# Routed experts: the last two tiles of each expert as one group of 256 moving rows

## What is computed

```python
h = _L0_tok_ref(x, ...)                    # gelu(codebook[x] @ W1 + b1) @ W2 + b2, 256 -> 1024 -> 256
h = h + _L0_attn_ref(_layernorm(h), ...)   # two minGRU layers, a scan over the sequence
h = h + _L0_ffn_ref(_layernorm(h), ...)    # below

def geglu(x, w1, w2, w3):
    return jax.nn.gelu(x @ w1, approximate=False) * (x @ w2) @ w3
shared = geglu(xf, w1s, w2s, w3s)
idx = jnp.argmax(xf @ Wg, axis=-1)         # one of 8 experts per token
for e in range(N_EXPERTS):
    y = geglu(xf, W1[e], W2[e], W3[e])
    final = final + jnp.where((idx == e)[:, None], y, 0.0)
```

## Time and profile before

| what | value |
|---|---|
| median of 3 runs | 494.27 us (494.14 to 494.92) |
| profiled execution: its own time | 494.67 us |
| profiled execution: span of the trace | 492.9 us |
| TensorE busy | 485.4 us, 98% |
| VectorE busy | 326.5 us, 66% |
| ScalarE busy | 248.9 us, 50% |
| GpSimd busy | 71.7 us, 15% |

### The profile page before, as it was taken

The page is one execution under the profiler, slowest core; times in us unless marked ns, Lnnn a source line. Parts: engine busy times, 40 slices in busy tenths (PEclk is TensorE's granted clock), DMA queues, the critical chain, the costliest instruction groups (busy, mean ns, idle before and its releaser), DMA issues.

```text
span 492.9 us, 8768 instructions
## 1 busy us (share of the span) xinstructions
PE 485.4 (98%) x2790; PEld 419.5 (85%) x2791; DVE 326.5 (66%) x538; ACT 248.9 (50%) x380; POOL 71.7 (15%) x85
## 2 busy tenths in 40 slices
PE   8999999999999999999999999999999999999997
PEld 7889888888888887888888788888888888888886
DVE  2567768669676778767544877843857476657364
ACT  3776774574663563534443765534554457254321
POOL 4431031011011001104350001011001000101120
PEclk9999999999999999999999999999999999999999
DMA  4852021001030004001354465530556074500352
GB/s 131 311 205 71 23 65 43 21 23 43 23 97 1 1 0 148 25 0 44 129 174 105 152 231 205 197 112 32 193 173 229 21 243 156 197 32 26 108 200 85
DMA packets 22986, 52.71 MB, mean 107 GB/s; under 512 B 6224, under 2 KB 16464, under 8 KB 18992
## 3 DMA queue, kind: packets, MB, share of 16 engines
q1 hardware_dynamic: 17296, 42.39, 25.1%
q0 software_dynamic: 2640, 7.22, 4.3%
q10 hardware_dynamic: 3024, 2.75, 1.9%
HBM read 41.85 MB, written 10.51 MB: 106 GB/s over the span
## 4 chain that ended last, share of the span: by engine, by line
PE 86%; DVE 4%; DMA 4%; ACT 3%; issue 2%; SPq 1%; POOL 0%; POOLq 0%; DVEq 0%
PE ps L258 23%; PE ps L259 22%; PE ps L260 22%; PE ps L733 8%; PE ps L736 4%; PE ps L745 3%; DMA stage<-w1s_in 2%; PE ps L640 1%; DVE stats L1107 1%; PE ps L558 1%; DMA q<-codebook_in,idx_sb 1%; PE ps L593 1%; PE ps L605 1%; DVE v_gate L1138 1%; ACT a_gate L893 1%
## 5 line engine op out<-in xcount | busy, mean ns | idle before, releaser
L1042 DVE TENSOR_TENSOR hT<-ps,hT 128x512 fp32r<-128x512 f32 x64 | 43.9, 686 | 34.6 <-ACT hT L833 17.6
L1385 DVE TENSOR_TENSOR w_slots<-stage,w_slots 128x2048 f32 x24 | 54.8, 2288 | 15.2 <-ACT w_slots L974 15.0
L258 PE MATMUL ps<-w_slots,xTp 128*128 (+1 forms) x160 | 64.0, 400 | 0.2
L260 PE MATMUL ps<-w_slots,xTp 128*128 (+1 forms) x160 | 62.4, 390 | 0.0
L259 PE MATMUL ps<-w_slots,xTp 128*128 (+1 forms) x160 | 62.4, 390 | 0.0
L733 PE MATMUL ps<-w_slots,gTp 128*128 (+1 forms) x160 | 58.9, 408 | 0.0
L432 POOL DMA_INDIRECT y_tokens<-y_row,row_ids x23 | 23.1, 1006 | 198.4 <-DVE y_row L1408 187.1
L844 ACT ACTIVATE hT<-ps 128x512 fp32r<-128x512 f32 x32 | 19.2, 598 | 54.5 <-DVE ps L1048 54.5
L1366 DVE TENSOR_TENSOR g_buf<-ps,gelu_buf 128x512 f32<-128x512 f32 x40 | 26.8, 685 | 28.1 <-PE ps L260 28.1
L736 PE MATMUL ps<-w_slots,gTp 128*128 (+1 forms) x160 | 44.9, 281 | 0.0
L974 ACT ACTIVATE w_slots<-stage 128x2048 f32 x21 | 40.3, 1918 | 3.9 <-issue 3.9
(11 more groups left out here) (185 smaller groups left out, 1218.1 us busy)
## 6 DMA issues: line engine op xcount, KB each, us to landing
stage<-ew_in SPq DMA_DIRECT2D x24, 1024.0 KB, 5.3
x_sorted<-zero_row SPq DMA_DIRECT2D x25, 128.5 KB, 2.5
x_row<-x_sorted ACTq DMA_DIRECT2D x21, 128.0 KB, 2.1
stage<-w1s_in SPq DMA_DIRECT2D x2, 1024.0 KB, 8.4
fetched<-y_tokens SPq DMA_DIRECT2D x4, 512.0 KB, 5.4
out_rows<-fetched SPq DMA_DIRECT2D x3, 512.0 KB, 2.9
first_stage<-tok_w_in SPq DMA_DIRECT2D x1, 1024.0 KB, 5.0
first_stage<-tok_w_in SPq DMA_DIRECT2D x4, 256.0 KB, 4.2
```

The lines of the kernel that those rows point to most:

```text
L258: pe.matmul(dst, lhs_hi, rhs_hi, start=start, stop=False, skip_group_check=shares_bank)
L260: return pe.matmul(dst, lhs_lo, rhs_hi, start=False, stop=stop, skip_group_check=shares_bank)
L1042: dve.tensor_tensor(hT[:, c % RING, 1, :], ps[:, bank, :], f32(hT[:, c % RING, 0, :]), ALU.subtract).then_inc(h_lo, 1)
L1385: dve.tensor_tensor(w_slots[:, bass.ds(to + (PART + c * WCH), WCH)], stage[:, c, :], f32(w_slots[:, bass.ds(to + c * WCH, WCH)]), ALU.subt ...
```

## The change

Each expert now has at least two tiles (`steps[:, :, 0:2] = -1`), and its last two are one window of 256 rows that is computed like the shared layer: weights stationary, 256 rows moving, the hidden values transposed from the start. A window has four pairs p of hidden chunks; `window_up` is 24 products of 256 columns for one p, `window_down` four pairs of a 512 and a 256 column product. Tiles beyond two (`count` of them, "singles") keep the old form, in nested conditions. The loop now runs over experts, two per turn, and turns behind the last up products, so that `window_down` of p = 2 and 3 is issued in the next expert. Addresses in `w_slots` are constants. Output rows have two buffers, and a new semaphore `y_free` tells VectorE that the store before the last has landed. `XT` becomes 2 x 8 + 14 = 30; GpSimd's loop runs over `XT` as before.

```diff
-    XT = TILES + EXPERTS - 1
+    MORE = TILES - 2
+    XT = 2 * EXPERTS + MORE
...
             def to_tokens(i):
                 pool.indirect_dma_start(
                     out=y_tokens, out_offset=bass.IndirectOffsetOnAxis(ap=row_ids[:, i:i + 1].bitcast(I32), axis=0),
-                    in_=y_row[:], in_offset=None,
+                    in_=y_rows[:, i % 2 * D:(i % 2 + 1) * D], in_offset=None,
                     bounds_check=(TILES + 1) * P - 1, oob_is_err=True).then_inc(y_stored, 16)
 
 
             pool.wait_ge(ids_land, 16)
             for i in range(XT):
-                pool.wait_ge(y_taken, i + 1)
+                pool.wait_ge(y_taken, i + 2)
                 if i:
                     pool.wait_ge(y_stored, i * 16)
+
+                pool.sem_inc(y_free, 1)
                 to_tokens(i)
 
 
...
+
+            w_parts = w_slots[:].rearrange("p (s h n) -> p s h n", s=2, h=2)
+
+            def window_up(e, p, odd):
+
+                slot = 0 if odd else SLOT
+                for w, done in enumerate((wa_ps, wb_ps)):
+                    for c in range(2):
+                        for k in range(KD):
+                            o = slot + w * WCH + k * HID + (2 * p + c) * P
+                            last = mm3(pe, ps[:, p % 2 * 2 + w, c * WINDOW:(c + 1) * WINDOW], w_slots[:, o:o + P],
+                                       w_slots[:, o + PART:o + PART + P], xW[:, odd, 0, k, :], xW[:, odd, 1, k, :],
+                                       k == 0, k == KD - 1)
+                    last.then_inc(done, 1)
+
+            def window_down(rounded, p, odd):
+
+                side = 0 if odd else 1
+                pe.wait_ge(w_lo, rounded)
+                for i in range(2):
+                    for c in range(2):
+                        o = 2 * WCH + (2 * p + c) * D
+                        cols = slice(c * WINDOW + i * P, c * WINDOW + (i + 1) * P)
+                        pe.matmul(ps[:, 4 + i, :].rearrange("p (h n) -> p h n", h=2), hW[:, p, 0, cols],
+                                  w_parts[:, side, :, o:o + D], start=p == 0 and c == 0, stop=False, skip_group_check=True)
+                        last = pe.matmul(ps[:, 4 + i, 0:D], hW[:, p, 1, cols], w_slots[:, side * SLOT + o:side * SLOT + o + D],
+                                         start=False, stop=p == PAIRS - 1 and c == 1, skip_group_check=True)
+                    if p == PAIRS - 1:
+                        last.then_inc(tile_done, 1)
+
...
+
+            def expert(e, odd):
+
+
+                opening = isinstance(e, int) and e == 0
+                if opening:
+                    chunk_down(AHEAD - 2, 0)
+                else:
+                    window_down(e * PAIRS - 1, PAIRS - 2, not odd)
+                s = ahead_of(pe, e)
+                m = rows_of(pe, e)
+                pe.wait_ge(pair_lo, e + 1)
+                if not opening:
+                    one_transposes(m)
+                pe.wait_ge(split_lo, e * 3 + 5)
+                window_up(e, 0, odd)
+                if opening:
+                    one_transposes(0)
+                    chunk_down(AHEAD - 1, 0)
+                else:
+                    window_down(e * PAIRS, PAIRS - 1, not odd)
+                count = singles_of(pe, e)
+                with pe.If(count > 0):
+                    if opening:
+                        pe.wait_ge(acc_taken, 2 * (2 * BLOCKS - 1))
+                    pe.wait_ge(one_lo, m + 1)
+                    single_half(s, 0, odd)
+
+                    pe.wait_ge(w_lo, e * PAIRS + 1)
+
+                    pe.wait_ge(y_taken, s + e * 2 + 1)
+                    single_half(s, 1, odd)
+                    with pe.If((count - 1) > 0):
+                        next_single(e, s, m, 1, odd)
+                        with pe.If((count - 2) > 0):
+                            with pe.Fori(2, MORE) as j:
+                                with pe.If((count - j) > 0):
+                                    next_single(e, s, m, j, odd)
+                    single_turn(last_of(pe, e), 0)
+                window_up(e, 1, odd)
+                with pe.If(count > 0):
+                    single_turn(last_of(pe, e), 1)
+                pe.wait_ge(w_lo, e * PAIRS + 1)
+                window_up(e, 2, odd)
+                if not (isinstance(e, int) and e == EXPERTS - 1):
+                    pe.wait_ge(one_lo, rows_of(pe, e + 1))
+                    pair_transposes(e + 1)
+                with pe.If(count > 0):
+                    last = last_of(pe, e)
+                    pe.wait_ge(split_lo, e * 3 + 6)
+                    pe.wait_ge(y_taken, s + count + e * 2)
+                    single_down(last, odd)
+                pe.wait_ge(split_lo, e * 3 + 6)
+                pe.wait_ge(y_taken, s + e * 2 + 1)
+                if opening:
+                    pe.wait_ge(acc_taken, 2 * (2 * BLOCKS - 1))
+                window_down(e * PAIRS + 1, 0, odd)
+                pe.wait_ge(w_lo, e * PAIRS + 2)
+                window_up(e, 3, odd)
+                window_down(e * PAIRS + 2, 1, odd)
+
+            pe.wait_ge(routed, 1)
             pe.wait_ge(h_lo, AHEAD - 1)
-            up_half(0, SLOT, 0)
-            chunk_down(AHEAD - 1, 0)
-            up_half(0, SLOT, 1)
-            row_transposes(1)
...
+
+            def expert(e, odd):
+                opening = isinstance(e, int) and e == 0
+                closing = isinstance(e, int) and e == EXPERTS - 1
+                m = rows_of(act, e)
+                if not opening:
+                    single_rows_hi(m)
+                if not closing:
+                    behind = window_behind(act, e)
+                    act.dma_start(x_pair[:], x_sorted[bass.ds(behind * P, WINDOW), 0:D].rearrange("(t p) d -> p t d", p=P)).then_inc(pair_land, 16)
+                count = singles_of(act, e)
+                s = ahead_of(act, e)
+                window_gelu(e, 0)
+                window_hi(e, 0)
+                if opening:
+                    single_rows_hi(0)
+                with act.If(count > 0):
+                    with act.If((count - 1) > 0):
+                        fetch_single(s + e * 2 + 1)
+                    single_gelu(s)
+                    with act.If((count - 1) > 0):
+                        next_single(s, m, 1)
+                        with act.If((count - 2) > 0):
+                            with act.Fori(2, MORE) as j:
+                                with act.If((count - j) > 0):
+                                    fetch_single(s + e * 2 + j)
+                                    next_single(s, m, j)
+                    single_hi(last_of(act, e), 0)
+                next_hi(e, 0, odd)
+                if not closing:
+                    fetch_single(s + count + e * 2 + 2)
+                window_gelu(e, 1)
+                window_hi(e, 1)
+                with act.If(count > 0):
+                    single_hi(last_of(act, e), 1)
+                next_hi(e, 1, odd)
+                window_gelu(e, 2)
+                window_hi(e, 2)
+                if not closing:
+                    window_rows_hi(e + 1, 1 - odd)
+                next_hi(e, 2, odd)
+                window_gelu(e, 3)
+                window_hi(e, 3)
 
             act.wait_ge(routed, 1)
...
-                step(dve.memset(steps[:, :, 0:1], -1.0))
+                step(dve.memset(steps[:, :, 0:2], -1.0))
...
+
+            def take_tile(done, bank, count=1):
+
+                dve.wait_ge(tile_done, done)
+
+                dve.wait_ge(y_free, done)
+                dve.tensor_reduce(y_rows[:, bass.ds(((done + 1) & 1) * D, D)], ps[:, bank, :].rearrange("p (h n) -> p n h", h=2), AX,
+                                  ALU.add).then_inc(y_taken, count)
...
+
+            def expert(e, odd):
+                opening = isinstance(e, int) and e == 0
+                m = rows_of(dve, e)
+                s = ahead_of(dve, e)
+                if not opening:
+                    single_rows_lo(m)
+                count = singles_of(dve, e)
+                window_gated(e, 0)
+                if opening:
                     add_rows(BLOCKS - 2)
-                    gated_half(i, 1)
-                    row_lo(i + 1)
-                    next_lo(0)
+                    single_rows_lo(0)
                 else:
-                    next_lo(0)
-                    gated_half(i, 1)
-                    row_lo(i + 1)
-                next_lo(1)
-                take_before()
-                gated_lo(i)
-                next_lo(2)
-
-            def take_routed(i, stored=None, count=1):
-                dve.wait_ge(tile_done, i + 1)
-                if stored is not None:
-                    dve.wait_ge(y_stored, stored)
-                dve.tensor_reduce(y_row[:], ps[:, 7, :].rearrange("p (h n) -> p n h", h=2), AX, ALU.add).then_inc(y_taken, count)
+                    take_tile(s + e * 2 - 1, 4)
+                    take_tile(s + e * 2, 5)
+                window_lo(e, 0)
+                with dve.If(count > 0):
```

(13 more changed lines are left out.)

362 lines of the change are left out of this document (200 added, 162 removed).

## The result

The changed kernel takes **511.88 us** (median, 511.62 to 512.4, 4 runs), the kernel before 494.25 beside it (494.14 to 494.92, 4 runs): ratio 1.035, 95% interval 1.0338 to 1.0363. The profiled execution of the changed kernel has a span of 509.9 us, that of before 492.9. The forecast was 509.2.

What follows compares the result with a forecast made beforehand. The prediction took TensorE, 98% busy, to bound the kernel before. From 494.67 us it took -8.3 (TensorE's work), +10.9 (the ring) and +11.9 (GpSimd's stores behind the end), giving 509.2 us, range 497 to 520.

Steps and rivals of the forecast that it cites:

- TensorE's work: Routed stage: eight windows at 17.7 us and four single tiles at 9.37, 179.1 for 187.4 us, so -8.3 us.
- the ring: ScalarE and VectorE chain of gatings, roundings and rests, 19.4 us per expert without singles; TensorE's waits add 10.9 us.
- the stage as a whole: Routed stage: 187.4 - 8.3 + 10.9 = 190.0 us, so +2.6 us.
- eleven steps: GpSimd's store tail, first to twelfth store: undisturbed steps of 3.22 us, others longer, sum 42.4 us.
- from the last store's start to the end: End of the kernel: the twelfth store starts at 503.8 and takes 0.97 us, so GpSimd ends at 504.8.
- The 1.1 us at `single_down`: Experts with singles: TensorE waits 1.1 us for the second half's rest, behind W1's rest and p = 1.
- Its upper bound: GpSimd's store tail: remaining steps all at 4.1 us and a wait for the last landing, about +17 us.
- The first: Routed stage and end: the ring costs nothing, the stores do; 498.3 us, chance 10%.
- The third: Routed stage and end: GpSimd's tail is hidden but the ring holds; 497.3 us, chance 5%.
- The second: Tail hidden and ring not deciding: 486.4 us at store steps up to 2.7, between 491.3; chance 6%.
- The fourth: TensorE's expert loop: some dozen jumps each stop it for one instruction fetch of 1.0 us; 521 us, chance 15%.
- The sum of waits of some 11 us: Sign on TensorE: its waits for hW's and gTp's rests come to some 11 us in all.

Runs made afterwards that it cites:

- the last run: Changed kernel with conditional stores, VectorE's weight rests one position later, and no code for singles in expert 0 on TensorE: 486.92 us, ratio 0.9847.
- the run without skip but with the ring: Changed kernel with 20 stores, and TensorE's list for expert 0 without the code for singles and its jump: 492.0 us, ratio 0.9955.
- the two other kernels that end so: Changed kernel with 25 stores in place of 30, 496.72 us; kernel before with 30 stores in place of 23, 508.88 us.
- VectorE's new order: Changed kernel with 20 stores, and VectorE's rests of W1 and W2 one pair of chunks later: 488.36 us, ratio 0.9888.

## Why the prediction was right, and where its steps were off

The sign, the place and the size were right: the time is 2.7 us above the forecast and well inside the range. The steps, in us:

| step | predicted | measured |
|---|---|---|
| TensorE's work in the stage | -8.3 | -8.9 |
| the ring's waits, without a stop | +10.9 | +6.3 |
| stops at branches, without the ring | 0 | +2.3 |
| ring and stops together | +10.9 | +6.5 |
| the stage as a whole | +2.6 | -2.4 |
| first of the last twelve stores starts at | 464.0 | 460.14 |
| eleven steps | 42.4 | 43.4 |
| from the last store's start to the end | 0.97 | 6.36 |
| span | 507.4 | 509.9 |

The first four rows come from stages: 192.55 before, 183.65 with neither ring nor stop, 189.95 with the ring alone, 185.94 with the stop alone and 190.12 with both, as the change was made.

**TensorE's work** is the stage of the last run, 183.65, against 192.55 before. Every part of it stood as costed: 24 products of 256 columns take 2.88 us, a window expert without waits 17.8 us from up product to up product (17.7 predicted), one with a single 27.0.

**The ring** is as long as worked out, 19.5 us; what it cost was sized too high, by 4.6 us. Expert by expert, the run without skip but with the ring against the one with neither, first product to first product:

| expert | 0 | 1 | 2 | 3 | 4 | 5 | 6 | 7 |
|---|---|---|---|---|---|---|---|---|
| predicted | 0.5 | 1.8 | 2.5 | 0.5 | 2.1 | 0.5 | 2.1 | 0.9 |
| measured | 0.6 | 1.7 | 1.0 | 0.2 | 0.9 | 0.2 | 0.9 | 0.7 |

The failing step is the layout of the lists in the experts with singles. The 1.1 us at `single_down` was put down three times and doesn't exist: that function's down products run 2.90 us without a gap (332.58 to 335.48 in the changed kernel), since the second half's rest is needed only at its fifth hidden chunk, 1.5 us in. The waits at the first single were right: 0.9 to 1.0 us in each of experts 2, 4 and 6 for 0.8 and 0.2. Experts 0 and 1 were right as well. In the changed kernel itself expert 1 takes 18.60 us and waits 0.8, not 1.7, because the stop in expert 0 had let the ring catch up. The two losses overlap there: 6.3 and 2.3 apart, 6.5 together. The prediction had a stop as a rival only, and no term for such an overlap.

**The end** was the second failing step, in the other direction. The prediction ended the span with the last store's 0.97 us on GpSimd; it goes on 6.36 us from its start, and 5.9 and 6.4 in the two other kernels that end so. The row of line 94 says what holds it, a DRAIN on GpSimd from 503.31 us on, 6.34 us long. The trace of the kernel before has it too, hidden behind the rest of the kernel:

```profile
L85 POOLq DRAIN  x1: 5802/5802/5802, 475.9 to 475.9; - x1
```

The prediction could have read its price there. Its upper bound had "a wait for the last landing" in it and should have been the choice, and even that (2.4 us to landing here) is too short. Summed up, in us against the forecast: the stage -5.0, its start +0.3, from its end to the first store +0.9 (3.3 for 2.4), the steps +1.0, the end +5.4, together +2.6. That the forecast came within 2.7 us is partly luck, as the two large errors nearly cancel; that GpSimd's tail decides is not.

**The stores' steps** came out as the pattern of the earlier trace rows had it: 3.22 undisturbed, 6.90 over the fetch, eleven together 1.0 us longer. The formula of the Trainium skill (DMA: Bandwidth & Descriptors, section "Anatomy of one DMA"), 2.3 us for 128 KB, is the price of one DMA, and the trace agrees with it as that: an undisturbed store takes 2.4 us from issue to landing. The prediction set it beside a step, which is something else. Where each store waits for the landing of the last, another 0.8 us pass until the next starts; no step here is under 3.2, and at 2.3 a step the tail would have been nearly hidden (an estimate: 460.14 + 11 x 2.3 + 6.36 = 491.8).

**Rivals.** The first (no ring) is refuted by VectorE's new order: 5.4 us, of which 4.3 are the stage. The third (the tail hidden, the ring not, 497.3) is refuted for the change as made, where the tail costs 18.1 us; the runs with 20 and with conditional stores are its case, 493.8 and 493.9. The second needs both out of the way by store steps of up to 2.7 us, and no step was under 3.2; with both mended by other means the time is 489.7, 3.3 above its 486.4. The fourth, branches, is true of two branches, worth 0.4 us with the ring in place and 2.3 without it, not of a dozen stops of 1.0 each. It isn't a price per jump. The instruction queue q8 fetches at 270.3, 273.4, 280.7, 290.4, 294.3, 306.0, 323.5 and 335.4 us, 16 KB each, and then not until 438.2, while the loop turns back twice and skips the code for singles in experts 3 and 5. At least part of this queue is TensorE's code, since it has 22 fetches and not 24 when the code for singles in expert 0 is gone from TensorE's list alone. The DMA queues of 340 to 430 us have no row for q8:

```profile
q1 hardware_dynamic: 1666, 12.08, 37.7%
q10 hardware_dynamic: 1664, 1.57, 5.9%
q0 software_dynamic: 480, 1.31, 3.7%
q14 instruction: 1, 0.01, 0.0%
```

So TensorE's code stays at hand once it was fetched. What the stop waits for can be told from the records. In the changed kernel one fetch runs from 270.34 to 271.23, while the branch is under way, and the branch ends at 272.72, 1.49 us behind it. In all eight kernels that have this skip the slow branch ends 1.48 to 1.50 us behind the end of such a fetch, and the slow one in expert 1 ends 1.33 to 1.41 us behind the end of another; the branches of the loop's second and third turns in the changed kernel, with no fetch beside them, take 0.07 to 0.22 us. By these times the stop is the fetch of the code, and its last 1.5 us lie behind the packet. (The 0.3 us in the expectation of the run without the skip is a misreading: no fetch ends there.)

The Trainium skill (Runtime: NRT & Kernel Launch, section "Instruction fetch mechanics") has two statements on this: that a taken branch out of the two page window stops the engine for a fetch, and that TensorE's instruction memory is 128 KiB where most others have 32. The two slow branches agree with a stop for a fetch. The traces are in keeping with the size, since 8 fetches of 16 KB serve expert 0 and the whole loop, and not with a two page window for TensorE: five of them fall into the loop's first turn, and the next two turns need none.

Of the signs that the prediction named, the last store behind TensorE's end, GpSimd in the chain, and 1.44 us for twelve 256 column products (24 in 2.88) are there. The sum of waits of some 11 us and 19 us for every window expert are not: the window experts of the loop take 18.6, 18.0 and 18.0. Of its signs of being wrong, one is there: an idle stretch of TensorE behind a branch that no semaphore ends. (VectorE is idle for 1.48 us ahead of one gating of expert 1, too, but for ScalarE's gelu, as the chain has it.)

## What to carry to other kernels

When a change raises a worst-case bound (here `XT`), look for every loop that is unrolled over it on a slow, serial engine: a padded store costs as much as a real one, and it costs it at the very end. Where two engines feed each other in order, walk the ring from start to start and compare it with the bound engine's time; moving a rest one position later was worth as much here as halving the work. Two idle times on one path need not add up: removing one lets the engine run into the other, so measure each with the other gone. A saving on the bound engine is only banked once both of these are out of its way, so test the mends apart before judging the form.

## What the runs showed of the hardware that was not expected

- **The end behind a GpSimd store is long.** The last store's packets move between 505.0 and 505.6 us, and 506 to 510 shows none:

```profile
DMA packets 0, 0.00 MB, mean 0 GB/s; under 512 B 0, under 2 KB 0, under 8 KB 0
```

  yet the span goes on to 509.9, and GpSimd's DRAIN with it (503.3 to 509.65). Behind SyncE's last writes the last packet ends at 491.5 and the span at 492.3, 0.8 us later (the kernel with 20 stores). What GpSimd does in these 4.3 us beyond the name DRAIN the trace doesn't say.
- **Code of a loop is not fetched again** on TensorE (no fetch between 335.4 and 438.2 us), but a branch that needs a fetch ends some 1.5 us behind its packet. The two such branches here cost 0.4 us when removed with the ring in place and 2.3 with the ring mended.
- **The start of the stage moves by up to 2 us** (266.7 to 268.8) between kernels that differ only in GpSimd's or VectorE's list behind it, with waits for `res` (up to 0.3, or 1.0 to 1.1 us) that come and go. Each is one profiled execution, and eleven executions of the kernel with 20 stores spread over 1.7 us, so this may be the spread of executions. Differences of 1 us between such kernels shouldn't be put down to the edited stage without comparing the stage itself.
